# A graph edge stage on blocks of 128 nodes instead of two times 64, with a ring of 24 turns of gathered rows

## The chip, the core and the metric

The kernel runs on one core of a Trainium2 chip. The metric is the device time of one execution in microseconds (us), as a median of three runs. The engines are TensorE (PE, matmuls into PSUM; PEld is its weight load), VectorE (DVE), ScalarE (ACT), GpSimd (POOL) and SyncE (SP, which issues DMAs).

## What is computed

One layer of a graph network with 6250 nodes of 256 features and 206,250 edges, sorted by target node: graph attention with 8 heads, plus a linear-attention branch, plus a soft mixture of 8 two-layer experts. The change touches the attention over edges and what reads its sums:

```python
h = (x @ W.T).reshape(n, H, D)
h_src, h_dst = h[src], h[dst]
alpha = einsum('ehd,hd->eh', h_src, a_src) + einsum('ehd,hd->eh', h_dst, a_dst)
enc = relu(edge_attr @ edge_W.T + edge_b).reshape(-1, H, D)
alpha = alpha + sum(enc * h_dst, axis=-1)
alpha = where(alpha >= 0, alpha, 0.2 * alpha)
amax = segment_max(alpha, dst, n)
ex = exp(alpha - amax[dst])
denom = segment_sum(ex, dst, n)
attn = ex / maximum(denom[dst], 1e-10)
out = segment_sum(h_src * attn[..., None], dst, n)
...
x = x + gnn(xn) + mix(xn)
x = x + ffn(layernorm(x))        # 8 experts, weighted by a softmax gate
```

## The kernel before

The program is a row of stages with a barrier between them: start (layer norm, node features `h`, the plan of the edges), KV and mix (the linear attention), edges, combine, experts.

The edges are cut into groups of 256 (`GE`). Nodes are cut into blocks of 64 (`WN`), 98 of them (`NJ`). A **step** is one group with one block; a plan made on the chip in the start stage lists the steps so that each group meets each block that its targets lie in. A **turn** is two steps, 512 edges; there are 452 turns (`D`), and eight turns are a **window** (57 of them) with one softmax pass. For each turn the following is done, all loops written out:

- SP loads the rows `h_dst` of the two blocks (`table`, bf16 in three parts that add up to fp32; the third part of 64 rows is laid out as two halves of the columns, one on partitions 0 to 63, one on 64 to 127), every second turn the edges' targets (`relb`) and features (`feat`). POOL gathers `h_src` with four indirect DMAs of 128 rows (`rows`), unless the turn is one of the 124 whose rows were gathered in earlier stages and are loaded by SP.
- DVE makes the one-hot matrix of targets (`hot`, L1826); PE multiplies it with the table (`spread_out`, L1652 and L1656) into `ps_d`, encodes the edge features (L1641) into `ps_f`, which ACT rectifies (L1734); DVE multiplies the two (L1837); PE reduces by head (L1669).
- Eleven turns later (`LAG`) the softmax weights of the window exist. ACT builds a one-hot matrix of 128 edges by 64 nodes four times (`one_hot`, L1779, L1781), DVE weighs the gathered rows (L1920), PE adds them up per node (`aggregate`): edges of the first group go to PSUM partitions 0 to 63 and 64 to 127 in turn, as do those of the second, since 64 nodes fill half of the output. So the sums of a block lie in two halves (bands) that combine adds later. The first step's sum is brought in from SBUF by a matmul with the identity (L1688), except in the first turn of a window, and written back by ACT (`put_back`, L1787); the second step's is added by DVE (`add`, L1913). Both write `sums`, and the next turn's aggregate waits for both.
- The ring of gathered rows holds 15 turns (`R`). POOL waits with turn `d` for the aggregate of turn `d - 15` and for the encoding of turn `d - 5`.

The order on each engine is that of the loops over `tau`: on PE table products, encode, aggregate of turn `tau - 12`, reduce of turn `tau`.

Combine reads `sums` through a matmul with `band_sum` (L2223), divides, adds the residual, and lays out `x` transposed (L2207) with the gate's logits (L2213). The experts' weights (`W1`, `W2`, `Wo`) are loaded over `sums`, when its last band sum is done (L2046).

## Time and profile before

| | us |
|---|---|
| median of three runs | 4003.45 |
| lowest, highest | 4001.85, 4003.85 |
| span of the profiled execution | 4846.5 |
| its start, KV and mix stages | 1027 |
| its edge stage | 2677 |
| its combine stage | 123 |
| its experts | 1019 |

Of the profiled execution only its span is known, from the first to the last instruction. It is 843 us above the median, a fifth: the durations of the profile's instructions hold, but its waits need not all exist in a run without the profiler. In the rows further below a time is in us from the span's start, a mean is in ns, "xN" counts records, and a matmul of fp32 leaves two records. `[2.00 <-DVE ...]` is the engine's idle time before a row and what ended it. Matmuls are pipelined and their ends are modelled, so what a group costs is best taken from start to start.

### The profile page before, as it was taken

How to read it: one execution, taken by the hardware profiler on the slowest of the kernel's cores; microseconds unless marked ns; L12 is line 12 of the kernel's file. 1: busy time of each engine (PE TensorE's matmuls, PEld its weight loads, DVE VectorE, ACT ScalarE, POOL GpSimd, SP SyncE). 2: the span in 40 equal slices, each digit the busy share in tenths (PEclk: the TensorE clock that was granted, in tenths of full speed). 3: DMA queues.
4: the chain of work that ended last, by engine and by line, in shares of the span. 5: the costliest groups of instructions: out<-in, count | busy, mean ns of one | idle time of the engine just before them, and what ended most of it. 6: DMA issues, size and time to landing. Idle time of an engine off the chain costs nothing. (4 is left out here: it accounts for less than half of the span.)

```text
span 4846.5 us, 80424 instructions
## 1 busy us (share of the span) xinstructions
PE 4087.7 (84%) x22764; PEld 1897.1 (39%) x22765; DVE 2700.2 (56%) x5470; ACT 2291.3 (47%) x6074; POOL 1780.1 (37%) x1859
## 2 busy tenths in 40 slices
PE   5699988957888887788887878878887999999999
PEld 3333322312333333333333333333333666666666
DVE  7566723336666666676666666667666333333333
ACT  4444445524555555555555555555554433333332
POOL 3255555644454445444444444445440000000000
PEclk8799989976888888888888887888887799999999
DMA  7555556655555555555555555555552100000000
GB/s 216 160 165 162 164 177 201 210 156 154 161 168 165 158 165 164 162 168 168 159 162 152 163 157 161 162 159 168 164 162 67 61 8 1 8 8 8 8 8 8
DMA packets 378173, 629.74 MB, mean 130 GB/s; under 512 B 83912, under 2 KB 245063, under 8 KB 377536
## 3 DMA queue, kind: packets, MB, share of 16 engines
q1 hardware_dynamic: 277266, 356.80, 23.4%
q0 software_dynamic: 93408, 257.23, 19.5%
q10 hardware_dynamic: 7104, 11.01, 0.7%
q8 instruction: 179, 2.93, 0.2%
q14 instruction: 216, 1.77, 0.1%
HBM read 520.59 MB, written 104.12 MB: 129 GB/s over the span
## 5 line engine op out<-in xcount | busy, mean ns | idle before, releaser
L1629 POOL DMA_INDIRECT s_rows<-scratch_src_rows,s_idx_w x1312 | 1257.6, 959 | 1367.6 <-PE s_ps_a L1692 563.3
L1837 DVE SCALAR_TENSOR_TENSOR s_enc<-s_enc,s_a_dst,s_ps_d 128x512 f32<-128x512 f32 x904 | 634.9, 741 | 313.3 <-DMA p_feats<-in_edge_f,p_tcol_i 160.8
L1734 ACT ACTIVATE s_enc<-s_ps_f 128x1024 f32<-128x1024 f32 x452 | 459.5, 1017 | 516.6 <-remote 265.5
L1692 PE MATMUL s_ps_a<-s_rows,s_hot_e 128*64 128x264 f32 x3616 | 647.1, 490 | 44.9 <-DVE s_rows L1920 32.4
L2285 DVE SCALAR_TENSOR_TENSOR kx_y_all<-e_ps_o,kx_gate,kx_y_all 128x256 f32 (+1 forms) x392 | 173.5, 480 | 684.2 <-PE e_ps_o L2340 684.2
L1920 DVE TENSOR_TENSOR s_rows<-s_rows,s_ps_x 128x1024 f32<-128x1024 f32 x452 | 545.7, 1207 | 13.6 <-ACT s_a_w L1765 8.7
L1688 PE MATMUL s_ps_a<-ke_sums,k_ident 128*128 x790 | 341.0, 520 | 217.1 <-DVE ke_sums L1913 123.6
L1913 DVE TENSOR_TENSOR ke_sums<-s_ps_a,ke_sums 128x264 f32 x509 | 218.3, 429 | 505.3 <-remote 263.9
L1669 PE MATMUL s_ps_s<-s_enc,s_head_sum 128*32 128x256 f32 x3616 | 353.7, 469 | 152.9 <-DVE s_enc L1837 121.2
L1779 ACT ACTIVATE s_hot_e<-k_iota_row,s_rel_w 128x64 f32<-128x64 f32 x1808 | 480.5, 339 | 0.0
L1787 ACT COPY ke_sums<-s_ps_a 128x264 f32 x395 | 148.6, 376 | 552.5 <-remote 337.8
L2299 ACT ACTIVATE ke_sums<-e_ps,kx_b,kx_g 128x448 f32<-128x448 f32 x224 | 162.1, 724 | 512.9 <-PE e_ps L2319 512.9
L1692 PEld LDWEIGHTS s_ps_a<-s_rows,s_hot_e 128*64 128x64 f32 x3616 | 263.0, 163 | 360.2 <-issue 264.5
L2319 PE MATMUL e_ps<-kx_xT,ke_sums 128*128 (+1 forms) x896 | 347.9, 542 | 6.2 <-PEq L180 6.2
L2340 PE MATMUL e_ps_o<-ke_sums 128*128 128x256 f32 x1568 | 347.6, 379 | 0.0
L2329 PE MATMUL e_ps<-ke_sums 128*128 128x448 f32 x896 | 345.9, 539 | 0.0
L1641 PE MATMUL s_ps_f<-s_feat,k_w_rows 30*128 30x512 bf16 x904 | 304.0, 419 | 27.7 <-DMA s_feat<-scratch_step_parts 14.6
L1656 PE MATMUL s_ps_d<-s_hot,s_table 128*128 128x256 bf16 x1808 | 321.7, 308 | 0.0
L2340 PEld LDWEIGHTS e_ps_o<-ke_sums 128*128 128x128 f32 x1568 | 297.7, 190 | 58.6 <-issue 20.9
L1091 POOL DMA_INDIRECT n_rows<-scratch_src_rows,n_idx x248 | 235.0, 947 | 207.0 <-PE n_ps_g L948 107.5
L1195 POOL DMA_INDIRECT m_rows<-scratch_src_rows,m_idx x248 | 235.7, 951 | 174.7 <-issue 64.6
L1688 PEld LDWEIGHTS s_ps_a<-ke_sums,k_ident 128*128 128x128 f32 x790 | 139.0, 220 | 373.5 <-issue 370.6
(280 smaller groups left out, 5259.0 us busy)
## 6 DMA issues: line engine op xcount, KB each, us to landing
s_table<-scratch_dst_parts SPq DMA_DIRECT2D x904, 96.0 KB
s_rows<-scratch_pre_rows SPq DMA_DIRECT2D x124, 528.0 KB
s_relb<-scratch_rel_rows SPq DMA_DIRECT2D x226, 256.0 KB
scratch_pre_rows<-n_rows SPq DMA_DIRECT2D x62, 528.0 KB
scratch_pre_rows<-m_rows SPq DMA_DIRECT2D x62, 528.0 KB
s_rows<-scratch_src_rows,s_idx_w POOLq DMA_INDIRECT x1312
s_feat<-scratch_step_parts SPq DMA_DIRECT2D x226, 54.0 KB
s_pen_w<-scratch_pen_rows SPq DMA_DIRECT2D x228, 48.1 KB
```

The source lines that it names most:

```text
L1629: pool.indirect_dma_start(out=rows[:, d % R, m, :], out_offset=None, in_=scr["src_table"], in_offset=bass.IndirectOffsetOnAxis(ap=idx_w[:, ...
L1656: last = PE.matmul(ps_d[:, c, sub * GE:(sub + 1) * GE], table[:, u, sub, c * P:(c + 1) * P], hot[:, v, sub * GE:(sub + 1) * GE], start=Fal ...
L1669: last = PE.matmul(ps_s[32 * b:32 * (b + 1), :], head_sum[:, 28 - 4 * k:60 - 4 * k], enc[:, d % 2, c, sub * GE:(sub + 1) * GE], start=(k = ...
L1688: PE.matmul(ps_a[:, 0, 0:SRC_W], keep["ident"][:], sums[:, bass.ds(j, 1), :].rearrange("p o w -> p (o w)"), start=True, stop=False, skip_g ...
L1692: last = PE.matmul(ps_a[t * WN:(t + 1) * WN, sub, 0:SRC_W], hot_e[:, d % 3, 2 * sub + t, :], rows[:, d % R, 2 * sub + t, :], start=(sub == ...
L1734: A.activation(enc[:, d % 2], ps_f[:], ACT.Relu).then_inc(enc_made, 1)
L1779: A.activation(hot_e[:, d % 3, m, :], keep["iota_row"][:, 0:WN], ACT.Abs, bias=rel_w[:, w % 3, k * TD + m:k * TD + m + 1]).then_inc(dist_m ...
L1837: V.scalar_tensor_tensor(out=enc[:, d % 2, c, :], in0=enc[:, d % 2, c, :], scalar=a_dst[:, c:c + 1], in1=ps_d[:, c, :], op0=ALU.add, op1=A ...
L1920: V.tensor_tensor(v, v, by.unsqueeze(3).to_broadcast([P, TD, H, HD]), ALU.mult).then_inc(weighed, 1)
L2319: last = nc.tensor.matmul(ps[q][:, 0:W], w["W1"][:, e, c, m * P:(m + 1) * P], keep["xT"][:, c, bass.ds(i * 2 * W + hf * W, W)], start=(c = ...
L2329: last = nc.tensor.matmul(ps[q][:, 0:W], w["W2"][:, e, c, m * P:(m + 1) * P], h1[:, c, hf * W:(hf + 1) * W], start=(c == 0), stop=(c == 1))
L2340: last = nc.tensor.matmul(ps_o[q][:, r, :], h2[:, c, b * P:(b + 1) * P], w["Wo"][:, e, c, :], start=(c == 0), stop=(c == 1))
```

## The change

Blocks are of 128 nodes, 49 of them (`NJ`). A turn is one double group of 512 edges with one block, so both its steps share the block, and the plan is made for double groups; there are 452 turns as before. What follows from it:

- The table is stored and loaded as 128 rows of 768 columns: three parts of 256. The two loads per turn become one. The products are six matmuls of 128 rows by 512 columns.
- Aggregate is four matmuls of 128 edges by 128 nodes into one of two PSUM banks in turn (`ps_a[:, d % 2]`). There is no reload from `sums` and no `put_back`; DVE adds the bank to `sums`, once per turn. Aggregate of turn `d` waits for the addition of turn `d - 2`. The one-hot matrices are 128 wide.
- Reduce moves: turn `tau - 1` is reduced after the table products of turn `tau`. On DVE the scores step moves behind `spreader`.
- The ring is 24 turns deep, and POOL waits for nothing but the ring's slot.
- `sums` holds 49 blocks instead of 98. Combine needs no band sum, divides in place, and turns four tiles ahead; the weights have memory of their own and are loaded at its start. `bo` and the experts' scratch stay on `sums`.

```diff
-WN = P // 2
+WN = P
...
-    NJ = 2 * NT
-    T = -(-E // GE)
-    D = -(-(T + NJ - 1) // 4) * 2
+    NJ = NT
+    T = 2 * -(-E // (2 * GE))
+    D = -(-(T // 2 + NJ - 1) // 2) * 2
...
-    R = 15
+    R = 24
...
-                    for sub in range(2):
-                        i = KS + 2 * k + sub
-                        j = sp.value_load(turns_w[0:1, w % 4, i:i + 1], min_val=0, max_val=NJ - 1)
-                        if sub == 0:
-                            wait(sp, spread[1], d - RL + 1)
-                        sp.dma_start(table[:, u, sub, :], row(scr["dst_parts"], j).rearrange("o c n w -> (o c n) w")).then_inc(table_in[u], 16)
+                    j = sp.value_load(turns_w[0:1, w % 4, k:k + 1], min_val=0, max_val=NJ - 1)
+                    wait(sp, spread[1], d - RL + 1)
+                    sp.dma_start(table[:, u].rearrange("p a w -> p (a w)"), row(scr["dst_parts"], j).rearrange("o n w -> (o n) w")).then_inc(table_in[u], 16)
...
-                    wait(pool, summed[1], d - R + 1)
-                    wait(pool, enc_made, d - 4)
+                    wait(pool, summed, d - R + 1)
...
-                    for sub in range(2):
-                        for c in range(2):
-                            PE.matmul(ps_d[:, c, sub * GE:(sub + 1) * GE], table[c * 64:(c + 1) * 64, u, sub, C:HALF],
-                                      hot[c * 64:(c + 1) * 64, v, sub * GE:(sub + 1) * GE], start=(sub == 0), stop=False, skip_group_check=True)
-                    for c in range(2):
-                        for sub in range(2):
-                            last = PE.matmul(ps_d[:, c, sub * GE:(sub + 1) * GE], table[:, u, sub, c * P:(c + 1) * P],
-                                             hot[:, v, sub * GE:(sub + 1) * GE], start=False, stop=True, skip_group_check=True)
-                        last.then_inc(spread[c], 1)
+                        PE.matmul(ps_d[:, c, :], table[:, u, c, C:HALF], hot[:, v, :], start=True, stop=False)
+                        PE.matmul(ps_d[:, c, :], table[:, u, 1, c * P:(c + 1) * P], hot[:, v, :], start=False, stop=False)
+                        PE.matmul(ps_d[:, c, :], table[:, u, 0, c * P:(c + 1) * P], hot[:, v, :], start=False, stop=True).then_inc(spread[c], 1)
...
-                    wait(pe, added, 2 * d)
-                    if k > 0:
-                        PE.matmul(ps_a[:, 0, 0:SRC_W], keep["ident"][:], sums[:, bass.ds(j, 1), :].rearrange("p o w -> p (o w)"),
-                                  start=True, stop=False, skip_group_check=True)
-                    for sub in range(2):
-                        for t in range(TG):
-                            last = PE.matmul(ps_a[t * WN:(t + 1) * WN, sub, 0:SRC_W], hot_e[:, d % 3, 2 * sub + t, :], rows[:, d % R, 2 * sub + t, :],
-                                             start=(sub == 1 or k == 0), stop=True, skip_group_check=True)
-                        last.then_inc(summed[sub], 1)
+                    wait(pe, added, d - 1)
+                    for m in range(TD):
+                        last = PE.matmul(ps_a[:, d % 2, 0:SRC_W], hot_e[:, d % 3, m, :], rows[:, d % R, m, :], start=(m == 0), stop=(m == TD - 1))
+                    last.then_inc(summed, 1)
...
+                    if 0 < tau <= D:
+                        reduce(tau - 1)
...
-                    if tau < D:
-                        reduce(tau)
...
-                        A.activation(hot_e[:, d % 3, m, :], keep["iota_row"][:, 0:WN], ACT.Abs, bias=rel_w[:, w % 3, k * TD + m:k * TD + m + 1]).then_inc(dist_made, 1)
+                        A.activation(hot_e[:, d % 3, m, :], keep["iota_row"][:], ACT.Abs, bias=rel_w[:, w % 3, k * TD + m:k * TD + m + 1]).then_inc(dist_made, 1)
...
-                    V.tensor_tensor(y, ps_a[:, sub, 0:SRC_W], y, ALU.add).then_inc(added, 1)
+                    V.tensor_tensor(y, ps_a[:, d % 2, 0:SRC_W], y, ALU.add).then_inc(added, 1)
...
-                for u in range(R):
-                    sp.wait_ge(banded[u], len(range(u, NT, R)))
```

How a turn stands on PE, in the middle of a window. Before, from aggregate to the next turn's aggregate (L1652 and L1656 are the table products, L1641 encode, L1682 the load of the block's number, L1688 the reload):

```order
L1692 MATMUL s_ps_a<-s_rows,s_hot_e 64x264 x4
L1669 MATMUL s_ps_s<-s_enc,s_head_sum 32x256 x4
L1652 MATMUL s_ps_d<-s_hot,s_table 128x256 x4
L1656 MATMUL s_ps_d<-s_hot,s_table 128x256 x4
L1641 MATMUL s_ps_f<-s_feat,k_w_rows 128x512 x2
L1682 TENSOR_LOAD s_turns_w
L1682 ISA x2
L1688 ISA
L1688 MATMUL s_ps_a<-ke_sums,k_ident 128x264
L1692 MATMUL s_ps_a<-s_rows,s_hot_e 64x264 x4
```

After (L1635 to L1637 are the table products, L1648 reduce, L1626 encode, L1664 aggregate):

```order
L1664 MATMUL s_ps_a<-s_rows,s_hot_e 128x264 x4
L1635 MATMUL s_ps_d<-s_hot,s_table 128x512
L1636 MATMUL s_ps_d<-s_hot,s_table 128x512
L1637 MATMUL s_ps_d<-s_hot,s_table 128x512
L1635 MATMUL s_ps_d<-s_hot,s_table 128x512
L1636 MATMUL s_ps_d<-s_hot,s_table 128x512
L1637 MATMUL s_ps_d<-s_hot,s_table 128x512
L1648 MATMUL s_ps_s<-s_enc,s_head_sum 32x256 x4
L1626 MATMUL s_ps_f<-s_feat,k_w_rows 128x512 x2
L1664 MATMUL s_ps_a<-s_rows,s_hot_e 128x264 x4
```

The products are six rows of 512 columns, reduce stands behind them, and the load of a number and the reload are gone; aggregate's output is 128 wide.

On ACT, one turn before (L1785 loads the block's number for the write-back L1787):

```order
L1734 ACTIVATE s_enc<-s_ps_f 128x1024
L1785 TENSOR_LOAD s_turns_w
L1785 ISA x2
L1787 ISA
L1787 COPY ke_sums<-s_ps_a 128x264
L1745 COPY s_a_win<-s_rows 128x2x4x4
L1771 COPY s_rows<-s_a_w 128x32
L1779 ACTIVATE s_hot_e<-k_iota_row,s_rel_w 128x64 x4
L1781 ACTIVATE s_hot_e<-s_hot_e,s_one 128x256
```

and after (L1705 is the rectifier, L1716 and L1742 the copies, L1750 and L1752 the one-hot matrices):

```order
L1705 ACTIVATE s_enc<-s_ps_f 128x1024
L1716 COPY s_a_win<-s_rows 128x2x4x4
L1742 COPY s_rows<-s_a_w 128x32
L1750 ACTIVATE s_hot_e<-k_iota_row,s_rel_w 128x128 x4
L1752 ACTIVATE s_hot_e<-s_hot_e,s_one 128x512
```

The write-back and its number are gone, and the one-hot rows are 128 and 512 wide instead of 64 and 256.

On SP at the beginning of combine, before, the last small loads and the five last loads of `x` are followed by the weights over `sums`, and a wait for the last band sum stands between them; after, nothing stands between them:

```order
L2041 DMA kx_m<-in_m 128x16
L2041 DMA kx_v<-in_v 128x16
L2036 DMA kx_y_all<-scratch_x_mix 128x7x256 x5
L2046 DMA ke_sums<-in_W 128x512 x2
L2046 DMA ke_sums<-in_Wo 128x512
```

```order
L1990 DMA kx_m<-in_m 128x16
L1990 DMA kx_v<-in_v 128x16
L1985 DMA kx_y_all<-scratch_x_mix 128x7x256 x5
L1993 DMA kx_weights<-in_W 128x512 x2
L1993 DMA kx_weights<-in_Wo 128x512
```

What moved is the wait, and the place that the weights go to.

## Rows read from the trace of the kernel before

**Rows 1.** The page's first part: busy time, share of the span, instructions.

```profile
PE 4087.7 (84%) x22764; PEld 1897.1 (39%) x22765; DVE 2700.2 (56%) x5470; ACT 2291.3 (47%) x6074; POOL 1780.1 (37%) x1859
```

**Rows 2.** Stretches by stage: us, busy per engine, granted clock, DMA share, GB/s.

```profile
0.00:1027.00 1027.00, 841.77 (x5574) 333.86 (x5575) 539.65 (x1016) 471.89 (x1219) 522.52 (x547) 0.93 0.58 181
1027.00:3704.00 2677.00, 2137.97 (x13340) 860.27 (x13340) 1763.50 (x3359) 1449.86 (x4297) 1257.57 (x1312) 0.81 0.55 158
3704.00:3827.00 123.00, 94.18 (x491) 64.40 (x492) 68.29 (x313) 45.46 (x110) 0.00 (x0) 0.65 0.34 114
3827.00:4846.00 1019.00, 1013.75 (x3360) 638.56 (x3359) 328.79 (x784) 324.11 (x448) 0.00 (x0) 1.00 0.02 6
```

**Rows 3.** Timeline of PE: start, duration, line, tiles; one turn at full clock.

```profile
3258.94 1.11 PE L1692 MATMUL s_ps_a<-s_rows,s_hot_e 128*64 128x264 f32 x8
3259.99 0.64 PE L1669 MATMUL s_ps_s<-s_enc,s_head_sum 128*32 128x256 f32 x8
3260.55 0.39 PE L1652 MATMUL s_ps_d<-s_hot,s_table 64*128 64x256 bf16 x4
3260.88 0.61 PE L1656 MATMUL s_ps_d<-s_hot,s_table 128*128 128x256 bf16 x4
3261.42 0.60 PE L1641 MATMUL s_ps_f<-s_feat,k_w_rows 30*128 30x512 bf16 x2
3261.95 0.71 PE L1688 MATMUL s_ps_a<-ke_sums,k_ident 128*128 x2
3262.60 1.11 PE L1692 MATMUL s_ps_a<-s_rows,s_hot_e 128*64 128x264 f32 x8
```

**Rows 4.** Timeline of PE, the window's own steps, and the tail's first.

```profile
3635.04 0.71 PE L1676 MATMUL s_ps_s<-k_ident,s_a_win 128*128 128x128 f32 x4 [2.08 <-issue]
...
3648.06 0.30 PE L1715 MATMUL s_ps_x<-s_carry,s_head_row 8*128 8x32 f32 x2
...
3653.35 0.71 PE L1722 MATMUL s_ps_x<-s_perm,s_prob 128*128 128x128 f32 x4
3653.99 0.38 PE L1725 MATMUL s_ps_x<-s_gain,s_ones 8*128 8x8 f32 x2
...
3656.09 1.11 PE L1692 MATMUL s_ps_a<-s_rows,s_hot_e 128*64 128x264 f32 x8 [1.15 <-DVE s_rows L1920]
```

**Rows 5.** Groups, 1700 to 3500 us: busy, mean ns, idle before them by releaser.

```profile
L1629 POOL DMA_INDIRECT s_rows<-scratch_src_rows,s_idx_w x909 | 872.4, 960 | 925.3 <-PE s_ps_a L1692 385.6 <-issue 382.1 <-remote 135.3
...
L1734 ACT ACTIVATE s_enc<-s_ps_f 128x1024 f32<-128x1024 f32 x312 | 317.1, 1016 | 303.7 <-remote 147.1 <-PE s_ps_f L1641 124.9 <-issue 30.7
...
L1688 PE MATMUL s_ps_a<-ke_sums,k_ident 128*128 x546 | 233.7, 516 | 146.1 <-DVE ke_sums L1913 83.6 <-issue 45.4 <-ACT s_hot_e L1781 5.7
...
L1781 ACT ACTIVATE s_hot_e<-s_hot_e,s_one 128x256 f32<-128x256 f32 x313 | 158.9, 508 | 10.2
...
L1787 ACT COPY ke_sums<-s_ps_a 128x264 f32 x274 | 103.1, 376 | 381.6 <-remote 240.0 <-PE s_ps_a L1692 106.9 <-issue 34.0
```

**Rows 6.** Timeline of PE in the experts: passes of 256 columns, fp32.

```profile
4003.32 6.21 PE L2340 MATMUL e_ps_o<-ke_sums 128*128 128x256 f32 x28
4009.36 6.18 PE L2319 MATMUL e_ps<-kx_xT,ke_sums 128*128 x16
```

**Rows 7.** Timeline of DVE, one turn of the edge stage.

```profile
2516.91 0.43 DVE L1913 TENSOR_TENSOR ke_sums<-s_ps_a,ke_sums 128x264 f32 x1 [1.78 <-remote]
2517.26 1.40 DVE L1837 SCALAR_TENSOR_TENSOR s_enc<-s_enc,s_a_dst,s_ps_d 128x512 f32<-128x512 f32 x2
...
2519.21 1.21 DVE L1920 TENSOR_TENSOR s_rows<-s_rows,s_ps_x 128x1024 f32<-128x1024 f32 x1
```

**Rows 8.** Timelines in combine: SP's first weights, PE's transposes after the last band sum.

```profile
3791.62 0.83 SPq L2046 DMA_DIRECT2D ke_sums<-in_W  x2
...
3796.22 0.67 PE L2207 MATMUL b_ps_t<-k_ident,kx_xT 128*128 128x128 f32 x2
...
3797.40 0.67 PE L2207 MATMUL b_ps_t<-k_ident,kx_xT 128*128 128x128 f32 x2
```

More of the change, by code:

```diff
@@ L1940, in _ @@
                         pick(w - 1)
-                    if tau >= LAG + 1 and win(tau - LAG - 1)[1] == 0:
-                        add(tau - LAG - 1, 0)
                     if chain == 0:
@@ L2214, in logits @@
                     last.then_inc(logits_done, 1)
-                pe.wait_ge(band_in, 16)
                 pe.wait_ge(w_in, 32)
-                for i in range(NT + LATE + 2):
+                for i in range(NT + 1):
                     if i < NT:
-                        u = i % R
-                        wait(pe, divided[u], i // R)
-                        for b in range(2):
-                            last = PE.matmul(ps_n[u][b * WN:(b + 1) * WN, 0:SRC_W], band_sum[:], sums[:, 2 * i + b, :], start=True, stop=True)
-                        last.then_inc(banded[u], 1)
-                    if 0 <= i - LATE < NT:
-                        turn(i - LATE)
-                    if 0 <= i - LATE - 1 < NT:
-                        logits(i - LATE - 1)
+                        turn(i)
+                    if i > 0:
+                        logits(i - 1)
         s.free()
```

218 lines of the change are left out of this document (92 added, 126 removed).

## The prediction

> **What bounds the kernel now.** I read the page first [rows 1]: the span of the profiled execution is 4846.5 us and TensorE (PE) is the engine with the most busy time. That span is 843 us above the median of 4003.45 us. No clock or chain of the timed runs is shown, so the profile gives durations, and the median has to be rebuilt from them. The table of stretches [rows 2] cuts the span into four: start, KV and mix stages (1027 us), edge stage (2677 us), combine (123 us), experts (1019 us). In the experts PE is busy for 1013.75 of 1019 us at a granted clock of 1.00: this stretch has nothing to lose in a profile, so it takes 1019 us in the timed runs too. The missing 843 us must come out of the first two. In the edge stage PE is busy 80% at a clock of 0.81, in the first stretch 82% at 0.93.
>
> How far can they shrink? The first stretch has 842 us of busy PE; at full clock that is 842 x 0.93 = 783 us, its least. So the edge stage of the timed runs lies between 4003 - 1019 - 123 - 1027 = 1834 us and 4003 - 1019 - 123 - 783 = 2078 us, where the trace has 2677 us. The next step is what PE must do there. One turn at full clock with no gap [rows 3], start to start: aggregate (L1692) 1.05 us, reduce (L1669) 0.56, the two table products (L1652, L1656) 0.33 and 0.54, encode (L1641) 0.53, the reload of the sums through the identity (L1688) 0.65: 3.66 us. The reload is left out in one turn of eight. Once in eight turns come the softmax steps [rows 4]: L1722 0.64 us (3653.35 to 3653.99), L1676 of the same form as much, L1725 0.38, L1715 0.30 and L1711, its like, as much, 2.26 in all. PE's floor is 452 x 3.66 - 57 x 0.65 + 57 x 2.26 = **1746 us**. Ramp and tail stand outside: from 3656.09 [rows 4] to the stage's end at 3704 only aggregates are left, 48 us, and I take some 70 us for both ends. So floor and ends, 1816 us, sit just under the least that the median allows, 1834. DVE is the next engine: 1763.5 / 452 = 3.90 us per turn [rows 2]. So the edge stage in the timed runs is bound by PE near full clock (2.4 GHz; 0.5 in the table would be 1.2), with DVE close behind. For one value I share the 843 us as the excess over PE's least: 2677 - 1816 = 861 us in the edge stage, 1027 - 783 = 244 us in the first stretch, so 657 us and 186 us. That makes the edge stage **2020 us** in the timed runs, 204 us above floor and ends, and the first stretch 841 us.
>
> What the excess of the profiled stage is can be seen in part [rows 5]: PE waits before the reload for the sum that DVE writes back (83.6 of 146.1 us), and ACT's write-back (L1787) waits 240 us for something that the trace doesn't show ("remote"). Three quarters of it must be absent from the timed runs; they have no room for it.
>
> **The change, part by part.**
> Table products: 8 matmuls become 6. Before, the third part of the table was multiplied in pairs of 64 rows that run side by side: 4 matmuls of 256 columns take 0.33 us, while 4 of 128 rows take 0.54 [rows 3]. The difference, 0.21 us, is 512 columns, and leaves 0.12 us for the change of kind. After, all six are 128 rows by 512 columns, one after the other: 3072 columns x 0.21/512 = 1.26, and 0.12 gives 1.38 us against 0.87. Bounds: 1.26 with no change-over, and 1.59 as three times the encode (two matmuls of 512 columns in 0.53).
> Aggregate: 4 fp32 matmuls of 64 output columns, in pairs side by side, took 1.05 us, and the reload 0.65. After there is no reload, but four matmuls of 128 output columns that cannot share the array. The nearest rows are the experts' [rows 6]: 28 passes of 256 columns, fp32, 128 x 128, from 4003.32 to 4009.36, 0.2157 us each. A matmul is two passes (the x8 for four), so eight passes of 264 columns take 8 x 0.2157 x 264/256 = 1.78, with 0.17 for the change of kind (1.05 less four such passes' time, 0.89, is 0.16) 1.95 us. Bounds: 1.78, and 2.6 as four times the reload's own 0.65. I take 1.95, since the experts' rows are the same kind of matmul in a row.
> Reduce and encode stay: 0.56 + 0.53. A turn is then 1.38 + 1.95 + 1.09 = **4.42 us** against 3.66 (3.01 without reload). PE's floor: 452 x 4.42 + 57 x 2.26 = **2127 us**, 381 us more.
> The waits: the reload's wait for DVE is gone, the aggregate now waits for the addition of two turns ago, and ACT loses the write-back with its register load. These are worth at most what stood above floor and ends, 204 us. I keep a third, 68 us, for waits that the change leaves (the softmax steps' chain, loads), between 0 and 204. The stage is then 2127 + 70 + 68 = **2265 us**. Reduce now stands behind the next turn's table products, so it no longer waits for DVE's product of the same turn; the table products still wait for the product before them, which has PE's 3.0 us of other work to get done.
> DVE: multiply (1.40 us for two), weigh (1.21) and add (0.43) [rows 7] stay as they are; it loses 57 additions, 25 us, under the cover of PE's 4.7 us per turn. ACT: 1449.9 / 452 = 3.21 us per turn [rows 2]. The one-hot rows go from 64 to 128 columns, four times, and their relu (L1781) from 256 to 512. L1781 takes 508 ns for 256 columns and L1734 1016 ns for 1024 [rows 5], 0.66 ns a column, so 512 more columns cost 0.34 us; L1787's 0.376 us goes, seven times in eight. Even, and hidden.
> GpSimd: 1312 gathers as before at 0.96 us busy [rows 5]; even at 1.25 us each they need 1640 us. They may now run twelve turns ahead instead of three or four. No row shows ACT waiting for gathered rows, so the deeper ring has nothing to win: 0. SP: one table load of 192 KB per turn instead of two of 96, one register load less: hidden.
> Combine: 123 us. The experts' weights were loaded only after the last band sum, from 3791.62 [rows 8], and the experts start at 3827. After, they go out at the start, and no band sums remain. Then PE's transpose and logits, 1.17 us per tile at low clock (3796.22 to 3797.40) [rows 8], or DVE's three passes of some 0.35 us, set 49 x 1.17 = 57 us; with 9 us until the first rows land, 7 us for the last group and 6 us for the gates 79 us. **44 us** saved; bounds 20 (the loads of weights, rows and bo in a row) and 60.
> Start: half as many stores of the table: below 5 us, taken as 0.
>
> **The sum.** 4003 - 2020 + 2265 - 44 = 4204, said as **4200 us**, 4.9% slower. For the profiled execution the same edits act on a stage that has 2 us per turn of disturbance; 4.70 us of PE's work plus one of that would be 2580 us, so its span may well fall, to some 4700 us, while the time rises. That is no contradiction: the profile has slack that the timed runs don't.
>
> **Rivals.**
> A, more of the same: the first stretch shrinks not at all and the edge stage was 1834 us, or the wide matmuls cost more. 4003 - 1834 + 2127 + 70 + 10 - 44 = 4332 with 10 us of waits left; with the products at 1.59 us on the forecast, 4204 + 95 = 4299. For it: ACT's and DVE's load. Against: [rows 6]. Chance 20%.
> B, loads: a DMA share of 0.55 [rows 2] might hide queues before the table, whose rows grow from 768 to 1536 bytes. The table is 904 x 96 KB, 89 MB of the stage's 2677 us x 158 GB/s = 423 MB, a fifth; halving its share frees at most 0.5 x 0.2 x 0.55 x 2677 = 147 us: 4057. Against: none of the waits of [rows 5] names it. Chance 10%.
> The Trainium skill, page Perfetto Trace Analysis, section DMA Optimizations, says that transfers under 2 KB carry a large overhead each and that batching helps where a kernel is bound by DMA. The trace here shows no such bound.
> C, faster: the clock. If the timed runs of before, too, run the edge stage well below full clock, because PE has gaps, the busier PE of after gets it back. That needs the first stretch to be shorter than its busy PE says (ends of matmuls are modelled), say 700 us; the edge stage is then 2161, that of after, with both matmul groups at their lower bounds (0.12 and 0.17 us less) and no waits left, 2127 - 131 + 70 = 2066, and combine saves 60: 4003 - 2161 + 2066 - 60 = 3848. With my own costs it decides for faster once the stage takes over 2265 - 44 = 2221 us before, 4.9 us per turn; I put it at 4.5. For: 0.81 in the profile against 1.00 in the unbroken experts. Chance 9%. Near the boundary nothing changes: 4%.
> The Trainium skill, page TensorE: Matmul & The Clock Gate, section What's actually happening, has the throttled state as the default and activity as what releases it; by that rule alone after would gain. The trace agrees on the direction [rows 2].
> D, the change doesn't do what it says: the deeper ring is used but meets no wait. That is in my sum already.
>
> **Chances.** Forecast 60%, A 18%, B 9%, C 9%, no change 4%. B and A are slower too, so slower by over 0.2% (about what a measurement of this kernel can tell from no change) has 0.87, within 0.2% 0.04, faster 0.09. The range leaves out C and the top of A where the costs add: 4050 (B; the edge stage at 2078 us before with no waits left gives 4078) to 4380.
>
> **What would show it.** In the profile of after: the six table products at 1.4 us and the aggregate at 1.95 us start to start at full clock; clock of the edge stage above 0.9 and PE busy over 90%; no wait of PE for the sums; ACT and DVE waiting for PE; the weights' loads ending before combine does, and combine at 80 us. Wrong if a turn without gaps takes under 4.1 us, or if matmuls of full width overlap.

## The result

The changed kernel takes **4097.37 us** (median of four runs, 4091.86 to 4100.63), the kernel before 4002.65 us beside it (four runs, 3986.76 to 4003.85). The ratio is 1.025, with a 95% interval of 1.023 to 1.027: slower, as forecast, and inside the range of 4050 to 4380, but with 95 us of loss instead of the forecast 200.

The first profile of the kernel before, which all rows ahead of the prediction come from, has a span a fifth longer than the timed runs. Its stages are as long as those of the runs further below on chips that take some 4780 us for this kernel (KV and mix 428 and 414 us, against 408 to 418 and 413 to 420 there, and 323 and 370 on a chip that takes 4000), so it was in all likelihood taken on such a chip. The comparison below is therefore with a new profile of the unchanged kernel (span 3993.7 us, median 3997.39 beside it), on a chip that takes 4000 us for it like the timed runs.

Stretches of the kernel before by stage (start, KV, mix, edges, combine, experts), to be read beside [rows 2]. The columns are window, length, busy us of PE, PEld, DVE, ACT and POOL with their counts, granted clock, DMA share and GB/s:

```profile
0.00:188.00 188.00, 95.90 (x372) 70.85 (x372) 119.53 (x334) 85.80 (x230) 52.87 (x51) 0.80 0.69 198
188.00:512.00 324.00, 306.20 (x2997) 129.80 (x2998) 285.17 (x409) 178.92 (x737) 235.46 (x248) 0.95 0.69 212
512.00:881.00 369.00, 348.03 (x2205) 119.61 (x2205) 131.32 (x273) 206.33 (x252) 235.24 (x248) 0.97 0.69 221
881.00:2846.00 1965.00, 1804.24 (x13340) 771.16 (x13340) 1744.37 (x3358) 1468.09 (x4297) 1270.58 (x1312) 0.95 0.75 215
2846.00:2973.00 127.00, 101.05 (x490) 68.93 (x490) 67.63 (x312) 45.57 (x110) 0.00 (x0) 0.61 0.34 110
2973.00:3993.00 1020.00, 1014.34 (x3360) 639.05 (x3360) 329.11 (x784) 324.10 (x448) 0.00 (x0) 1.00 0.02 6
```

The same six stretches of the changed kernel (span 4090.1 us):

```profile
0.00:164.00 164.00, 92.56 (x356) 65.70 (x356) 115.27 (x328) 86.28 (x230) 51.57 (x50) 0.82 0.73 226
164.00:486.00 322.00, 306.58 (x2998) 130.09 (x2998) 285.15 (x409) 179.10 (x737) 235.53 (x248) 0.96 0.69 213
486.00:851.00 365.00, 343.57 (x2205) 117.51 (x2205) 131.27 (x273) 206.37 (x252) 235.11 (x248) 0.99 0.69 223
851.00:2968.00 2117.00, 2091.74 (x11646) 1140.28 (x11646) 1739.75 (x3298) 1523.11 (x3902) 1261.42 (x1312) 0.99 0.68 199
2968.00:3070.00 102.00, 61.33 (x294) 57.76 (x294) 62.50 (x228) 45.17 (x110) 0.00 (x0) 0.52 0.41 137
3070.00:4090.00 1020.00, 1014.13 (x3360) 639.01 (x3360) 329.13 (x784) 324.57 (x448) 0.00 (x0) 1.00 0.02 6
```

So the loss has four parts: start 188 to 164 (-24 us), KV and mix 693 to 687 (-6), edges 1965 to 2117 (+152), combine 127 to 102 (-25). That is +97, and the spans differ by 96.4. In the edge stage of the changed kernel PE is busy for 2091.74 of 2117 us at a clock of 0.99. Before it was busy for 1804.24 of 1965 us (92%) at 0.95, with DVE at 89%. So PE has 287 us more to do and stands idle 135 us less, 25 us instead of 161: that is the +152.

Timeline of PE in the changed kernel (start, duration, line, tiles), one turn without a gap, to be read beside [rows 3]:

```profile
1501.49 0.38 PE L1635 MATMUL s_ps_d<-s_hot,s_table 128*128 128x512 bf16 x1
1501.70 0.38 PE L1636 MATMUL s_ps_d<-s_hot,s_table 128*128 128x512 bf16 x1
...
1502.57 0.38 PE L1637 MATMUL s_ps_d<-s_hot,s_table 128*128 128x512 bf16 x1
1502.88 0.64 PE L1648 MATMUL s_ps_s<-s_enc,s_head_sum 128*32 128x256 f32 x8
1503.45 0.60 PE L1626 MATMUL s_ps_f<-s_feat,k_w_rows 30*128 30x512 bf16 x2
1503.98 2.05 PE L1664 MATMUL s_ps_a<-s_rows,s_hot_e 128*128 128x264 f32 x8
1505.86 0.38 PE L1635 MATMUL s_ps_d<-s_hot,s_table 128*128 128x512 bf16 x1
```

From start to start: table products 1.39 us, reduce 0.57, encode 0.53, aggregate 1.88, in all 4.37 us. The softmax steps, once in eight turns, are shown in part here:

```profile
2894.52 0.61 PE L1695 MATMUL s_ps_x<-s_perm,s_prob 128*128 128x128 f32 x4
2895.06 0.38 PE L1698 MATMUL s_ps_x<-s_gain,s_ones 8*128 8x8 f32 x2
2895.38 0.39 PE L1635 MATMUL s_ps_d<-s_hot,s_table 128*128 128x512 bf16 x1
```

These two add 0.54 and 0.32 us. The others are taken from the distances of the aggregates of successive turns: the turn with L1655 is 0.65 us longer than 4.37, and those with L1684 and L1688 0.15 us each, so a window has 1.81 us of them. Eight turns then make 8 x 4.37 + 1.81 = 36.8 us, and the L1655 steps of successive windows stand 36.80 us apart on average in the middle of the stage: the turn is PE's own work and nothing else.

Who waited for whom between 900 and 2900 us (engine, line, what released it: us in total, times, longest), in the changed kernel:

```profile
POOL s_rows L1614 <- DMA s_idx_w<-scratch_edge_idx: 382.6, 51, 12.6
...
ACT s_enc L1705 <- PE s_ps_f L1626: 343.3, 324, 1.5
DVE ke_sums L1871 <- PE s_ps_a L1664: 205.4, 251, 1.5
```

and of PE alone, where this is the only row:

```profile
PE s_ps_x L1695 <- ACT s_prob L1729: 2.4, 1, 2.4
```

The kernel before, 900 to 2800 us, PE alone:

```profile
PE s_ps_a L1688 <- DVE ke_sums L1913: 56.0, 55, 1.0
PE s_ps_a L1688 <- issue: 38.5, 55, 0.7
PE s_ps_x L1711 <- DVE s_ends L1857: 15.7, 44, 2.2
PE s_ps_f L1641 <- DMA s_feat<-scratch_step_parts: 10.1, 15, 2.4
PE s_ps_s L1669 <- DVE s_enc L1837: 3.6, 7, 1.1
...
```

Before, PE stood for the sums ahead of the reload. After, nothing in 2000 us holds PE for more than 2.4 us, and ACT and DVE wait for PE. The "remote" waits of [rows 5] are in neither list.

### The profile page after: what moved, and what is told of

The parts are those of the page before. It is cut to its first block and busy times, and to the rows that moved or that the text cites. A ratio compares the mean times of both kernels' runs of the same rounds, so it can differ in the third digit from the quotient of the medians.

```text
span 4090.1 us, 69094 instructions
## 1 busy us (share of the span) xinstructions
PE 3909.9 (96%) x20859; PEld 2150.4 (53%) x20859; DVE 2663.1 (65%) x5320; ACT 2364.6 (58%) x5679; POOL 1783.6 (44%) x1858
## 5 line engine op out<-in xcount | busy, mean ns | idle before, releaser
L1664 PE MATMUL s_ps_a<-s_rows,s_hot_e 128*128 128x264 f32 x3616 | 927.1, 400 | 2.9 <-DVE s_rows L1878 2.9
L1664 PEld LDWEIGHTS s_ps_a<-s_rows,s_hot_e 128*128 128x128 f32 x3616 | 651.9, 190 | 239.3 <-issue 140.1
L1705 ACT ACTIVATE s_enc<-s_ps_f 128x1024 f32<-128x1024 f32 x452 | 463.0, 1024 | 394.6 <-PE s_ps_f L1626 386.2
L1750 ACT ACTIVATE s_hot_e<-k_iota_row,s_rel_w 128x128 f32<-128x128 f32 x1808 | 576.8, 391 | 2.4 <-PE s_ps_a L1664 2.3
L2260 PE MATMUL e_ps<-kx_xT,kx_weights 128*128 (+1 forms) x896 | 347.9, 542 | 6.1 <-PEq L180 6.1
L1635 PE MATMUL s_ps_d<-s_hot,s_table 128*128 128x512 bf16 x904 | 345.1, 382 | 4.4 <-DVE s_hot L1785 2.5
L2281 PE MATMUL e_ps_o<-kx_weights,ke_sums 128*128 128x256 f32 x1568 | 347.6, 379 | 0.0
L2270 PE MATMUL e_ps<-ke_sums,kx_weights 128*128 128x448 f32 x896 | 345.9, 539 | 0.0
L1637 PE MATMUL s_ps_d<-s_hot,s_table 128*128 128x512 bf16 x904 | 344.6, 381 | 0.0
L1636 PE MATMUL s_ps_d<-s_hot,s_table 128*128 128x512 bf16 x904 | 344.6, 381 | 0.0
L1752 ACT ACTIVATE s_hot_e<-s_hot_e,s_one 128x512 f32<-128x512 f32 x452 | 326.2, 722 | 14.7
L2281 PEld LDWEIGHTS e_ps_o<-kx_weights,ke_sums 128*128 128x128 f32 x1568 | 297.8, 190 | 58.6 <-issue 21.0
L1648 PE MATMUL s_ps_s<-s_enc,s_head_sum 128*32 128x256 f32 x3616 | 289.6, 392 | 0.0
L1626 PE MATMUL s_ps_f<-s_feat,k_w_rows 30*128 30x512 bf16 x904 | 272.1, 380 | 15.9 <-DMA s_feat<-scratch_step_parts 15.9
```

The lines of the kernel that those rows point to most:

```text
L1635: PE.matmul(ps_d[:, c, :], table[:, u, c, C:HALF], hot[:, v, :], start=True, stop=False)
L1636: PE.matmul(ps_d[:, c, :], table[:, u, 1, c * P:(c + 1) * P], hot[:, v, :], start=False, stop=False)
L1637: PE.matmul(ps_d[:, c, :], table[:, u, 0, c * P:(c + 1) * P], hot[:, v, :], start=False, stop=True).then_inc(spread[c], 1)
L1664: last = PE.matmul(ps_a[:, d % 2, 0:SRC_W], hot_e[:, d % 3, m, :], rows[:, d % R, m, :], start=(m == 0), stop=(m == TD - 1))
L1705: A.activation(enc[:, d % 2], ps_f[:], ACT.Relu).then_inc(enc_made, 1)
L1750: A.activation(hot_e[:, d % 3, m, :], keep["iota_row"][:], ACT.Abs, bias=rel_w[:, w % 3, k * TD + m:k * TD + m + 1]).then_inc(dist_made, 1)
```

## The experiments

The kernels ran in four series. The first (b_again to b_reduce_moved) had a chip that takes 3997 us for the kernel before, called undisturbed below; the second had another chip, that takes 4776 us for it, and the last two a third one, that takes 4784 and 4787 us. Their times are compared only with the kernel before beside them.

**The kernel before, once more.**

> The kernel before, unchanged, to see its chain in an execution as long as the timed ones. My account (the edge stage bound by PE with gaps): span about 4000 us, first stretch about 845 us, edge stage about 2018 us (4.45 us per turn), with PE busy over 90% of it at a clock above 0.9, and some 200 us above PE's floor of 1746 us plus 70 us of ends. Rival (the edge stage bound by DVE): DVE busy over 90% and PE under 85%.

Measured: 3995.53 us, span 3993.7, granted clock 0.946. The profile is the one shown above. The 843 us by which the first profile exceeded the median are no cost of the profiler: here the profiled run takes what the timed runs take. The two profiled spans differ by 853 us, of which 146 lie in the first three stages (1027 against 881) and 713 in the edge stage (2677 against 1964); combine has 4 us less.

**The ring back to 15 turns**, and POOL's second wait back:

```
-    R = 24
+    R = 15
...
                     wait(pool, summed, d - R + 1)
+                    wait(pool, enc_made, d - 4)
```

> The changed kernel with the ring at 15 turns and GpSimd's wait for the encoding put back. My account (no engine waits for gathered rows): within 5 us of the changed kernel's 4097 us. Rival (the deeper ring is what lets PE run without gaps): 50 us or more slower, with ACT waiting for rows in the trace.

Measured: 4096.13 us, ratio to the kernel before 1.024 (1.021 to 1.026), against 1.025 (1.023 to 1.027) with 24 turns. POOL's waits, 900 to 2900 us:

```profile
POOL s_rows L1615 <- issue: 461.0, 1135, 4.9
POOL s_rows L1615 <- PE s_ps_a L1665: 315.4, 123, 5.5
```

With 15 turns POOL waits 315 us for the aggregate to give a place free; with 24 it waits 383 us for the next window's indices instead. Of the gathered rows ACT waits for 10.4 us in the whole stage with 15 turns and 12.9 us with 24. The deeper ring is worth nothing here.

**Reduce back at the end of the turn**, in the changed kernel:

```
                     if tau < D:
                         spread_out(tau)
-                    if 0 < tau <= D:
-                        reduce(tau - 1)
...
+                    if tau < D:
+                        reduce(tau)
```

> The changed kernel with the reduce of a turn back at the end of that turn. My account: PE works 4.37 us per turn and DVE's product is there 2.9 us after the table products began, before PE reaches reduce, so nothing changes (within 10 us of 4097 us). Rival (the new place of reduce is what took PE's gaps away): 40 us or more slower, with PE waiting for DVE before reduce.

Measured: 4124.49 us, ratio 1.032 (1.029 to 1.034). Its edge stage is 2144 us, 28 more than the changed kernel's 2116. So reduce's new place is worth 27 us of the time. Neither account holds: it is more than 10 us, but PE waits for DVE before reduce once, for 0.3 us in all. Timeline of PE, one turn:

```profile
1509.62 2.05 PE L1664 MATMUL s_ps_a<-s_rows,s_hot_e 128*128 128x264 f32 x8
1511.60 0.64 PE L1648 MATMUL s_ps_s<-s_enc,s_head_sum 128*32 128x256 f32 x8
1512.17 0.39 PE L1635 MATMUL s_ps_d<-s_hot,s_table 128*128 128x512 bf16 x1
```

From aggregate to reduce it is 1.98 us, where aggregate to the table products takes 1.88 in the changed kernel; the turn is 4.48 us instead of 4.37. A change of shape costs this. Products and aggregate use the array as 128x128, reduce as 128x32, encode as 30x128, and going from one shape to another costs some 0.1 us: 0.31 us lie between the last product and reduce, 0.22 between two products. With reduce next to encode the shape changes three times in a turn, with reduce behind the aggregate four times. Over a window, in which the softmax steps give some of it back, it is 37.35 us against 36.80; 0.55 us for each of 57 windows is 31 us, against the 28 measured. So the stage follows PE's work, with no wait in between, on an undisturbed chip. (The waits list has 17 us before L1636 here; they stand where a record of L1635 is missing.)

**Reduce moved in the kernel before**, behind the next turn's table products, and nothing else of the change (DVE's `scores` goes behind `spreader`, as in the changed kernel):

```
                     if tau < D:
                         spread_out(tau)
+                    if 0 < tau <= D:
+                        reduce(tau - 1)
...
-                    if tau < D:
-                        reduce(tau)
```

> The kernel before with reduce moved behind the next turn's table products and DVE's scores behind the spreader, as in the change. If PE's gaps of before are waits for DVE's product of the same turn: 50 to 150 us faster than before. If they are waits for the sums' write-back: no change, within 20 us.

Measured: **3959.66 us**, ratio 0.990 (0.987 to 0.993): the least time of all on this chip, 1% under the kernel before and clear of the interval, and between what the two accounts gave (50 to 150 us, or under 20). The edge stage falls from 1964 to 1936 us. PE's waits, 900 to 2800 us:

```profile
PE s_ps_a L1688 <- DVE ke_sums L1913: 51.5, 60, 1.8
PE s_ps_a L1688 <- issue: 38.3, 57, 0.8
PE s_ps_d L1652 <- DVE s_hot L1826: 17.9, 56, 1.3
```

The waits for the sums stay. DVE is now busy 1753 of the stage's 1936 us, PE 1793. A turn without gaps takes 3.66 us with reduce in either place. Here aggregate uses the array as 128x64 and the first products as 64x128, so there are six changes of shape in a turn both ways. So the 28 us are not what the changed kernel loses with reduce late: PE's idle time falls from 161 to 143 us and its busy time by 11, at a clock of 0.96 instead of 0.95. This run also moves DVE's `scores`; how much each of the two moves gives was not tried.

**Half of the aggregate left out**, in the changed kernel, twice (two groups of edges of four are not summed):

```
-                    for m in range(TD):
+                    for m in range(TD // 2):
```

> The changed kernel, but the aggregate sums two of a turn's four groups of edges instead of four (the other two are left out of the sums; everything else runs as before). Theory (after is bound by PE's own work, turn after turn): the turn loses two of four matmuls of 128 x 264, 0.94 us of the 1.88 read from the trace of after, so PE's floor falls from 4.65 to 3.71 us per turn and DVE's 3.85 to 3.9 us per turn becomes the limit with waits at the seams: 4.0 to 4.2 us per turn, the edge stage falls from 2116 us to 1800 to 1900, the time from 4096 to 3790 to 3900. Rival (what is left beside PE is what counts: DVE, gathers or the rings, and PE only waits busily): under 100 us are gained.

> The kernel of a_half_sum unchanged (two of the four groups of edges are left out of the sums), once more, since the chip of that series took 4776 us for the kernel before. On a chip that takes about 4000 us for the kernel before, the theory (after is bound by PE's own work in every turn) gives 1800 to 1900 us for the edge stage against 2116 and 3790 to 3900 us in all; the rival, that something beside PE sets the turn, under 100 us of gain. On a chip that takes 4776, 4868 again.

Measured: 4868.06 us (ratio 1.017, 1.014 to 1.021) and 4879.56 us (1.021, 1.015 to 1.027), with edge stages of 2752 and 2752 us. The nearest to the full changed kernel on such a chip is the two-store variant below, with 2815 us. The aggregate takes 0.99 us from start to start where it is followed without a gap, instead of 1.88. So 0.89 us per turn less of PE's work, some 400 us, bought 63. As a test of the turn's bound on an undisturbed chip both runs failed, since neither had such a chip. They show that on the slower chips the edge stage is not bound by PE's work alone. Two of the waits of the second, 1100 to 2900 us:

```profile
ACT s_enc L1705 <- remote: 577.3, 73, 17.2
POOL s_rows L1614 <- DMA s_idx_w<-scratch_edge_idx: 395.5, 30, 18.7
```

**Encode in two groups of rows**, twice: the second matmul reads a copy of the weights' and features' 30 rows on partitions 32 to 61, so that the two can run side by side.

```
-    last = PE.matmul(ps_f[:, c, :], w_rows[:, c * P:(c + 1) * P], feat[:, d // 2 % RP, d % 2, :], start=True, stop=True)
+    last = PE.matmul(ps_f[:, c, :], w_rows[32 * c:32 * c + FR, c * P:(c + 1) * P], feat[32 * c:32 * c + FR, d // 2 % RP, d % 2, :], start=True, stop=True)
```

> The changed kernel with its whole computation; encode's two matmuls of 30 rows read from different partitions (rows 0 to 29 and a copy in rows 32 to 61), so that they can run side by side, as the pairs of 64 rows did in the kernel before. One more load of the 27 feature rows per two turns. Theory (every us of PE's turn counts): encode falls from 0.53 us to 0.31 (one matmul's time and the change of kind), 0.2 us x 452 = 95 us, at most 0.25 x 452 = 113: 3985 to 4010 us. Rival (the edge stage has DVE just behind PE): DVE needs 3.9 us of the 4.4 left, so the rival gives nothing back here; a third account, that two matmuls of 30 rows do not overlap: 4096, no change, and a load more.

> The kernel of a_encode_pair unchanged (encode's two matmuls in two groups of rows, whole computation), once more for the same reason. On a chip that takes about 4000 us for the kernel before: 0.2 us less in each of 452 turns, 3985 to 4020 us, if PE's work is the bound of after; 4096 if it is not. With DVE at 3.85 to 3.9 us of busy time per turn behind PE's 4.4, nothing else comes in first.

Measured: 4925.64 us (ratio 1.032, 1.028 to 1.035) and 4917.72 us (1.030, 1.024 to 1.036), edge stages of 2801 and 2788 us, 14 and 27 less than the two-store variant's. The time again says little there, but the turn can be read. Timeline of PE of the second run:

```profile
1511.29 0.39 PE L1629 MATMUL s_ps_f<-s_feat,k_w_rows 30*128 30x512 bf16 x2
1511.61 2.05 PE L1667 MATMUL s_ps_a<-s_rows,s_hot_e 128*128 128x264 f32 x8
...
1515.45 0.39 PE L1629 MATMUL s_ps_f<-s_feat,k_w_rows 30*128 30x512 bf16 x2
1515.77 2.05 PE L1667 MATMUL s_ps_a<-s_rows,s_hot_e 128*128 128x264 f32 x8
```

Encode takes 0.32 us from start to start instead of 0.53, and a turn without gaps 4.16 us instead of 4.37. The Trainium skill, page TensorEngine Tiling (Array Packing), section Key Properties, says that different tiles of the array can multiply in parallel; the trace agrees that the two overlap, with 0.21 us of the 0.53 gone. On an undisturbed chip, 452 turns of it should be worth 95 us; that is an estimate, no such run was had.

**Two stores per tile of the table** in the start stage of the changed kernel, in pieces of 768 bytes as before:

```
-    sp.dma_start(scr["dst_parts"][d], parts[:, d % RP].rearrange("p c w -> p (c w)")).then_inc(d_stored[d % RP], 16)
+    for c in range(2):
+        sp.dma_start(scr["dst_parts"][d].rearrange("n (c w) -> n c w", c=2)[:, c, :], parts[:, d % RP, c, :]).then_inc(d_stored[d % RP], 16)
```

> The changed kernel; in the first stage each tile of the table is stored in two pieces of 768 bytes a row by two transfers, as in the kernel before, instead of one of 1536 bytes. Account 1 (the first stage lost 25 us because ACT waits less for the stores: 31.8 us after, 47.9 before): the first stage goes from 163 back towards 180 us and the time up by 10 to 20 us. Account 2 (it lost them because the plan of the turns has half as many comparisons, indices and rows to make): the first stage stays within 4 us of 163.

Measured: the start stage takes 168.2 us (from its first instruction to that of KV), against 163.5 and 163.0 in the profiles of the changed kernel and its ring variant, and 160.4 to 164.8 in the other variants of it. ACT's wait for the stores, 31.4 us, does not rise. So both accounts miss a little: by this one execution the stores are worth 3 to 8 us of the 24, and the rest goes with the other edits of that stage. The plan has 98 blocks to compare before and 49 after; which of its steps brings it was not tried.

**PE's register load at the head of the turn**, in the kernel before with reduce moved:

```
+                    j = at(tau - LAG - 1)          # the load of the row's number, moved here from aggregate
                     if tau < D:
                         spread_out(tau)
```

> The kernel before with reduce moved (3959.7 us); PE also loads the register that names the reload's row at the head of the turn instead of right before the aggregate. Account 1 (the 38 us that PE stands before L1688 with no releaser are the register load's own time): they go, and since DVE is 0.3 us per turn behind, 15 to 38 us are gained: 3920 to 3945 us. Account 2 (PE's issue runs ahead anyway, or the time turns into a longer wait for DVE's sum): within 8 us of 3960.

Measured: 4758.11 us, ratio 0.996 (0.993 to 0.999). The chip is another than that of the 3959.7 us, so the time decides nothing, but the trace does. PE's rows at the reload (1100 to 3500 us of the span):

```profile
PE s_ps_a L1691 <- DVE ke_sums L1917: 70.8, 60, 2.8
...
PE s_ps_a L1691 <- issue: 58.1, 64, 2.6
```

The second looks like the row that the edit was made for (57 times in b_reduce_moved), but it stands elsewhere. In b_reduce_moved the idle time comes once per window, right behind the softmax step on `ends` (L1711 before), in 56 of 57 windows, 38 us in all:

```profile
1524.95 0.23 PE L1713 MATMUL s_ps_x<-s_ends,s_head_of 128*8 128x32 f32 x2
1525.91 0.71 PE L1688 MATMUL s_ps_a<-ke_sums,k_ident 128*128 x2 [0.73 <-issue]
```

With the load at the head of the turn it is gone there in all 56, in this run and in the next (the first profile of the kernel before, also disturbed, has idle time there in 44 of 56):

```profile
1550.26 0.23 PE L1717 MATMUL s_ps_x<-s_ends,s_head_of 128*8 128x32 f32 x2 [0.35 <-DVE s_ends L1861]
1550.57 0.71 PE L1691 MATMUL s_ps_a<-ke_sums,k_ident 128*128 x2
```

The rows with no releaser of this run stand behind encode instead, 62 times, and such rows are in the first profile of the kernel before too (33 times, 43 us), but not on the undisturbed chip (none in b_again). So account 1 is right about the cause: the 38 us are the register load. It shows once per window, in the turn whose wait for DVE's `ends` stands ahead of the load in PE's program. That the load runs ahead of PE's work in the other turns, and can't do so behind that wait, is argued and not shown. What moving it gains on an undisturbed chip was not measured.

**Both, and encode in two groups**, in the kernel before with reduce moved:

> The kernel before with reduce moved, the register load at the head of the turn, and encode's two matmuls in two groups of rows. Account 1 (before is held by PE's work, its register load and the wait for DVE's sum together, so each bit counts in part): 3900 to 3945 us on a chip that takes about 4000 for the kernel before. Account 2 (with reduce moved DVE's 3.85 to 3.9 us per turn is the bound, and what PE saves turns into waits for DVE): 3945 to 3965, no more than with reduce moved alone.

Measured: 4758.34 us, ratio 0.995 (0.993 to 0.998), the same as without the groups of rows. On this chip neither account can be told from the other.

**No gathers** in the edge stage of the changed kernel. Every turn is loaded by SP; the rows are others, so the sums are too.

```
-                    if is_pre(dims, d):
-                        q = pre_before(dims, d)
+                    if True:
+                        q = d
...
-    sp.dma_start(rows[:, d % R].rearrange("p m w -> p (m w)"), scr["pre_rows"][q]).then_inc(kept_in[q % RQ], 16)
+    sp.dma_start(rows[:, d % R].rearrange("p m w -> p (m w)"), scr["pre_rows"][q % dims["NP"]]).then_inc(kept_in[q % RQ], 16)
```

> The changed kernel without the gathers of the edge stage: the 1312 indirect loads of GpSimd are left out, and every turn takes its 528 KB of rows in one plain load of SyncE from the rows laid by before (124 of the 452 turns do that already), so the sums are of other rows; PE, DVE and ACT have the work of the changed kernel. Theory (the gathers cost the changed kernel nothing, as my sum has it with the ring at 0 and GpSimd's 1640 us hidden): on a chip that takes about 4000 us for the kernel before, 4075 to 4105 us and an edge stage of 2095 to 2125 us. On a chip that takes about 4780, where the edge stage of the changed kernel has 2815 us instead of 2116, there are two accounts: the gathers are what holds the engines up there (the stages without gathers, start, combine and experts, have the same length on both chips), and then the edge stage falls below 2300 us and the time below 4420; or the gathers are not the cause, and the edge stage stays above 2700.

Measured: **4230.92 us** on a chip that takes 4787 for the kernel before, ratio 0.883 (0.879 to 0.886). The edge stage takes 2115.9 us (992.2 to 3108.1). On the undisturbed chip, with gathers, it took 2116.0. The table of three stretches (KV, mix, edges) of this run, with PE at a clock of 0.99 in the last:

```profile
164.00:577.00 413.00, 352.71 (x2998) 141.12 (x2998) 286.79 (x409) 175.40 (x738) 235.67 (x248) 0.94 0.53 166
577.00:996.00 419.00, 355.13 (x2205) 120.94 (x2205) 132.95 (x277) 206.13 (x252) 235.79 (x248) 0.95 0.61 195
996.00:3108.00 2112.00, 2091.55 (x11646) 1140.33 (x11646) 1733.51 (x3294) 1522.30 (x3902) 0.00 (x0) 0.99 0.62 199
```

And the edge stage of the two-store kernel, with gathers, on such a chip:

```profile
996.00:3811.00 2815.00, 2294.53 (x11646) 1217.09 (x11646) 1751.96 (x3298) 1509.80 (x3902) 1256.00 (x1312) 0.89 0.51 150
```

Without the gathers the edge stage is as long as on the undisturbed chip to 0.1 us. KV and mix, which still gather, are as long as in the other runs on such chips (413 and 419 us in the table, 322 and 365 on the undisturbed chip). The first account is shown: on these chips the engines are held up by the gathers. The run takes out POOL's instructions and the reads of scattered rows together, so which of the two does it isn't told apart. Between the ends of the two-store run's edge stage there are 69 stretches of over 1 us, 255 us together, in which PE, DVE and ACT all stand; the gathers' DMA queue moves 108 GB/s in them, against 64 over the stage, and SP's falls from 88 to 31. The changed kernel on the undisturbed chip has no such stretch.

The run also bears on the changed kernel itself. Two programs that share the work of PE, DVE and ACT, one with gathers and one without, take 2116 us for the stage, and PE is busy for all of the 1800 us from 1100 to 2900 in both. With the late reduce and the ring above, this shows that PE's own work is the bound of the changed kernel, and that gathers and ring add nothing to it.

## The prediction, point by point

**What bounds the kernel before.** Right in kind. I rebuilt the edge stage of the timed runs as 2020 us within 1834 to 2078; it is 1964. The first stretch is 881 us, not 841, combine 127, not 123. The excess went 713 to 146, where I had it 657 to 186. The 783 us that I called the least of the first stretch are none: PE is busy for only 750 us there. PE near full clock with DVE close behind is what the edge stage shows (0.95, 92% and 89%).

**The turn after.** Products 1.39 us (said 1.38), aggregate 1.88 (1.95), reduce 0.57 (0.56), encode 0.53 (0.53): 4.37 against 4.42. The way to the aggregate's price, from the experts' fp32 passes of [rows 6], held: eight passes of 264 columns give 1.78, and the change of kind cost 0.10, not 0.17. The softmax steps add 1.81 us per window, not 2.26: I had taken three of them at the length of their row and not from start to start. PE's floor by the measured parts is 452 x 4.37 + 57 x 1.81 = 2078 us.

**The ends and the waits: the terms that failed.** I added 70 us for ramp and tail and 68 us for waits left. The stage took 2116, 38 above the floor, so 138 us were given to what costs 38; PE is idle for 25 of these, and its first 116 us run at a clock of 0.89. Two errors. The 70 us were in large part counted twice: the aggregates that fill the tail are among the 452 turns of the floor already, so only what PE loses at the ends may be added. In the last 138 us of the stage PE is busy for 130.40. And I kept a third of the slack of before for waits, although the argument for none stood in the text: DVE's 3.9 us and ACT's 3.2 under PE's 4.4. From 967 to 2830 us PE is busy for all of the 1863 us. Of the 149 us between 2265 and 2116, 23 are the turn, 26 the softmax steps and 100 the ends and the waits. The 56 us of the stage before, 2020 against 1964, work the other way, so the difference of the two stages was forecast as 245 us and is 152. That the miss is not larger is luck, since two errors of the same sign, one in each stage, cancel in part.

**Reduce's place.** Said to end a wait for DVE's product; no price of its own. It is worth 27 us in the changed kernel, and there the reason given is wrong: no wait ends, but PE changes the shape of its array three times per turn instead of four. In the kernel before, together with the move of `scores`, it is worth 38 us (28 of them in the edge stage), by fewer gaps. I had it down as a detail; it is the one part of the change that pays in both.

**Combine.** 25 us saved, not 44. Timeline of PE at its start, after the change:

```profile
2989.46 1.09 PE L2155 MATMUL b_ps_t<-k_ident,kx_xT 128*128 128x128 f32 x4 [22.97 <-ACT kx_xT L2124]
2993.40 1.02 PE L2161 MATMUL b_ps_l<-b_wr,kx_xT 128*128 128x8 f32 x4 [2.86 <-ACT kx_xT L2128]
2994.28 0.67 PE L2155 MATMUL b_ps_t<-k_ident,kx_xT 128*128 128x128 f32 x2
...
2995.45 0.67 PE L2155 MATMUL b_ps_t<-k_ident,kx_xT 128*128 128x128 f32 x2
```

A tile takes the 1.17 us that I took (2994.28 to 2995.45, clock 0.52 in the stage). What I left out is that the first transpose needs the statistics of a whole group of seven tiles: it comes 21 us into the stage (2968.4), where I had 9 until the first rows land. And ACT normalises a group's seven tiles before it copies any, with 1.4 us of stall in six groups and 2.9 in the first, so that the transposes and logits take 75 us (to 3064) and not 57. The end takes 6 us, where I had 13 for the last group and the gates. 21 + 75 + 6 is 102. The weights' loads go out early, as said (from 2983 us), and hold nothing up.

**Start.** Taken as 0 and "below 5 us"; the stores are worth 3 to 8, near what was said. But the stage is 24 us shorter. I did not look at the plan, of whose comparisons and rows half as many are made; that this is what brings the rest is argued from the code and not shown.

**Ring, ACT, DVE, SP.** The ring is worth 0, as said. ACT's one-hot rows take 391 ns and 722 ns instead of 339 and 508 of before (0.21 us more for the second, where I had 0.34), and ACT ends up waiting 343 us for PE. DVE loses 57 additions, hidden.

**The sum** by measured terms: 3994 - 24 - 6 + 152 - 25 = 4091, the profiled span. By mine it was 0 + 245 - 44 = 201; the misses of the edge stage (93), start and mix (30) all went one way and combine's (19) the other.

**The profile's own span**: I said some 4700 for a disturbed execution. On an undisturbed chip it is 4090; on a disturbed one the nearest kernel has 4934. I had the stage of the profile fall from 2677 to 2580 us, as if the change took away most of the disturbance; it rises to 2815. The gathers hold the stage up by some 1.5 us per turn (699 / 452) on top of 4.68, much as before the change (713 / 452).

**Rivals.** A (wider matmuls dearer) and C (the clock pays for it) are out: turn 4.37, and before had a clock of 0.95 already, so there were 5% to win and not 19. The Trainium skill (page TensorE: Matmul & The Clock Gate, section What's actually happening) has activity release the throttle; the trace agrees on the direction, since the clock rose from 0.95 to 0.99 as PE's idle time went from 161 to 25 us, and that is in the 152. B (bigger rows per load) never met a wait: DMA's share fell from 0.75 to 0.68, and between 900 and 2900 us no engine waited for the table. D is true and cost nothing. A and B have 20% and 10% in their own paragraphs and 18% and 9% in the sum of chances.

## What to carry to other kernels

A matmul that fills half of the array's width may be the cheaper one if two of them run side by side: making it full width took out a reload of 0.65 us and put in 1.35 us. Matmuls of the same shape of the array belong side by side: one change less per turn was worth 27 us. When the engine at the bound is busy all the time, add only what it loses at the ends to its floor, and take every part of the floor from start to start. A row of idle time with the same name and nearly the same count after an edit need not be the same idle time: look at what stands before it. And before a profile is used for anything but durations, its span has to be held against the timed runs; a fifth too long was a sign of another chip, and most of the waits in it belonged to that.

## What the runs showed of the hardware

- The kernel before takes 4000 us on one chip and 4780 on two others, each of its runs within 1% of the median. The stages without gathers have the same length on both (start 160 to 168 us, combine 101 to 102, experts 1020 for the changed kernel and its variants); those with GpSimd's indirect loads get longer: KV from 322 us to between 408 and 418, mix from 365 to 370 us to between 413 and 420, edges from 2116 to 2815. With the gathers of the edge stage replaced by plain loads of the same size, that stage is back at 2115.9 us. What differs in the chips, and why a gather there stops other engines, the traces don't show: many of their waits are put down to "remote", and one gather's own row is 961 ns on the undisturbed chip and 957 ns on the other.
- Two matmuls of 30 rows and 512 columns, on partitions from 0 and from 32, take 0.32 us together against 0.53 one after the other.
- Eight fp32 passes of 264 columns on the full array take 1.88 us, and the eight passes with 64 output columns, in pairs side by side, that they replace took 1.05.
- Going from one shape of the array to another costs some 0.1 us (0.31 against 0.22 us behind a table product, 1.98 against 1.88 behind the aggregate, 0.53 against 0.44 behind encode).
- The load of a register on PE shows as 0.7 us of idle time in the one turn per window in which it stands behind a wait for DVE (56 of 57 windows), and in the others not, on the undisturbed chip.
